# Two of a head's three half-filled filter blocks share one block of 128 rows, with operand tiles made by transfers within SBUF

## What is computed

```python
x = x + _L0_conv_ref(_gn(x), gate_w, w1, w2, w3)         # experts
x = x + _L1_conv_ref(_gn(x), w3, w7, w15, w_mix)         # and two more like it
...
x_flat = x.reshape(b, l, h * d).transpose(0, 2, 1)
outs = [_causal_dwconv(x_flat, w) for w in (w3, w7, w15)]
y = jnp.concatenate(outs, axis=1)
y = y.reshape(b, h, n_scales * d, l).transpose(0, 3, 1, 2)
return jnp.einsum('blhm,dm->blhd', y, w_mix)
```

## Time and profile before

| | us |
|---|---|
| median of 3 runs | 1094.27 (1093.65 to 1095.57) |
| profiled execution: its own time | 1094.17 |
| its span in the profile | 1092.2 |
| PE (TensorE matmul) busy in the span | 1040.1 (95%) |
| DVE, ACT, POOL busy | 501.0, 318.4, 126.3 |

### The profile page before, as it was taken

The page is one execution under the profiler, slowest core; times in us unless marked ns, Lnnn a source line. Parts: engine busy times, 40 slices in busy tenths (PEclk is TensorE's granted clock), DMA queues, the critical chain, the costliest instruction groups (busy, mean ns, idle before and its releaser), DMA issues.

```text
span 1092.2 us, 14489 instructions
## 1 busy us (share of the span) xinstructions
PE 1040.1 (95%) x5315; PEld 870.7 (80%) x5316; DVE 501.0 (46%) x700; ACT 318.4 (29%) x435; POOL 126.3 (12%) x169
## 2 busy tenths in 40 slices
PE   5589999999999999999999999779999999999998
PEld 3278888888888888888888888668888988898887
DVE  4794154155136155245164372266236942587011
ACT  2412144144144244144144352114201320122122
POOL 2031111111111211111111122100000000000000
PEclk9859999999999999999999999979999999999999
DMA  8309216943972985953976949755373466436474
GB/s 346 126 20 340 48 29 241 390 158 145 389 253 68 399 320 213 393 183 116 410 269 259 392 149 400 241 216 186 128 231 132 148 231 224 148 117 246 153 222 116
DMA packets 69792, 240.16 MB, mean 220 GB/s; under 512 B 6272, under 2 KB 36096, under 8 KB 55360
## 3 DMA queue, kind: packets, MB, share of 16 engines
q1 hardware_dynamic: 61536, 216.62, 52.1%
q0 software_dynamic: 8080, 23.07, 9.0%
q10 hardware_dynamic: 144, 0.02, 0.0%
HBM read 136.15 MB, written 107.74 MB: 223 GB/s over the span
## 4 chain that ended last, share of the span: by engine, by line
PE 83%; DVE 7%; issue 4%; DMA 3%; SPq 1%; ACT 1%; POOLq 0%; DVEq 0%; ACTq 0%; POOL 0%
PE gate_ps L977 15%; PE up_ps L977 15%; PE y_ps L964 10%; PE head_ps L1466 9%; PE head_ps L1470 9%; PE head_ps L1467 9%; PE y_ps L967 5%; PE hT_ps L989 2%; PE xT_ps L954 1%; PE xT_ps L886 1%; SPq L409 1%; DMA block_row<-in_x,fetch 1%; DVE scaled L1267 1%; DVE split L1277 1%; PE turn_ps L1416 1%
## 5 line engine op out<-in xcount | busy, mean ns | idle before, releaser
L1466 PE MATMUL head_ps<-split,ring 128*128 128x256 f32 (+1 forms) x657 | 225.4, 343 | 1.4 <-ACT split L1158 1.2
L1470 PE MATMUL head_ps<-split,ring 128*128 128x256 f32 (+1 forms) x657 | 220.6, 336 | 0.0
L1467 PE MATMUL head_ps<-split,ring 128*128 128x256 f32 (+1 forms) x657 | 220.1, 335 | 0.0
L977 PE MATMUL gate_ps<-front 128*128 128x512 f32 x560 | 177.3, 398 | 1.8 <-DVE xT_lo L810 1.7
L977 PE MATMUL up_ps<-front 128*128 128x512 f32 x560 | 173.8, 392 | 0.0
L1466 PEld LDWEIGHTS head_ps<-split,ring 128*128 128x128 f32 x657 | 124.4, 189 | 15.4 <-issue 2.1
L1470 PEld LDWEIGHTS head_ps<-split,ring 128*128 128x128 f32 x657 | 124.3, 189 | 14.6
L1467 PEld LDWEIGHTS head_ps<-split,ring 128*128 128x128 f32 x657 | 124.6, 190 | 13.6
L827 DVE TENSOR_TENSOR hidden<-silu,up_ps 128x1024 f32<-128x1024 f32 x35 | 42.8, 1222 | 177.9 <-ACT silu L586 177.9
L977 PEld LDWEIGHTS up_ps<-front 128*128 128x128 f32 x560 | 105.7, 189 | 22.9
L977 PEld LDWEIGHTS gate_ps<-front 128*128 128x128 f32 x560 | 102.9, 189 | 22.2 <-DVE xT_lo L810 2.1
(11 more groups left out here) (189 smaller groups left out, 1164.7 us busy)
## 6 DMA issues: line engine op xcount, KB each, us to landing
filters<-rows SPq DMA_DIRECT2D x56, 1568.0 KB
w_raw<-in_w13T SPq DMA_DIRECT2D x32, 1024.0 KB, 7.1
ring<-filters SPq DMA_DIRECT2D x15, 1920.0 KB, 7.9
w_raw<-in_w2T SPq DMA_DIRECT2D x16, 1024.0 KB, 5.2
ring<-filters SPq DMA_DIRECT2D x21, 768.0 KB, 4.7
ring<-filters SPq DMA_DIRECT2D x12, 1152.0 KB, 6.0
rows<-in_x SPq DMA_DIRECT2D x4, 1024.0 KB, 8.1
rowed<-acc SPq DMA_DIRECT2D x4, 1024.0 KB, 6.1
```

Source lines behind the costliest of these rows:

```text
L977: last = nc.tensor.matmul(o[:, n, :], a[:, k, :], b[:, k, t, n * 512:(n + 1) * 512], start=(k == 0 and a is xT_hi and b is w13_hi), stop=( ...
L1466: nc.tensor.matmul(place, kernel_hi, x_hi, start=(u == 0 and a == 0), stop=False)
L1467: nc.tensor.matmul(place, kernel_lo, x_hi, start=False, stop=False)
L1470: last = nc.tensor.matmul(place, kernel_hi, x_lo, start=False, stop=(u == len(units) - 1 and a == windows(s) - 1))
```

## The change

A head's three units end with a half-filled block each. Two of them (units 0 and 1, for head 5 units 1 and 2, which have the same scale) give their last blocks to one block of 128 rows: the upper half of one filter block stays in partitions 64 to 127, that of the other is loaded into partitions 0 to 63. The moving operand of that block, `shared`, is put together in the same way from the two groups' `split`: partitions 64 to 127 of the one stay, those of the other go to 0 to 63. This is done by transfers from SBUF to SBUF, issued by POOL: 2 for a task of 512 columns, 4 for a task of 256. Four slots of `shared` are used in turn. Each head now has one block less, three matmuls; the shared block comes last in the task. SP issues two loads more for each head (the two halves of its shared block), and where the parts of a run are no longer equally long, one more. The ring has 36 places instead of 48, at new positions. DVE gets one more memset, of the zero columns of `shared`.

```diff
+def head_shared(h):
+    units = head_units(h)
+    return (0, 1) if units[0][0] == units[1][0] else (1, 2)
+
+def head_parts(h):
+    return [(s, j, windows(s) - (m in head_shared(h))) for m, (s, j) in enumerate(head_units(h))]
...
 def head_windows(h):
-    return sum(windows(s) for s, _ in head_units(h))
+    return sum(n for _, _, n in head_parts(h)) + 1
...
-RING = 48
-RING_PLACE = {11: 0, 12: 15, 6: 30, 13: 0, 14: 15, 15: 30, 10: 0, 7: 15, 8: 30, 9: 39, 0: 0, 1: 6, 2: 15, 3: 24, 4: 30, 5: 36}
+RING = 36
+RING_PLACE = {11: 0, 12: 14, 6: 28, 13: 0, 14: 14, 15: 0, 10: 14, 7: 28, 8: 0, 9: 16, 0: 8, 1: 24, 2: 0, 3: 14, 4: 19, 5: 28}
...
+SHARED = 4
+SHARED_AT = {h: i % SHARED for i, h in enumerate(HEAD_ORDER)}
+SHARED_PARTS = {None: (slice(0, 2),), 0: (slice(0, 1), slice(1, 2)), 1: (slice(0, 1), slice(1, 2))}
...
+        shared = sb("shared", [P, SHARED, 2, BATCH, LEAD + P], f32r)
...
+                at = (RING_PLACE[h] + head_windows(h) - 1) * 2 * P
+                for half, m in zip((1, 0), head_shared(h)):
+                    s, j, count = head_parts(h)[m]
+                    begin = SCALE_AT[s] + count * P
+                    sp.dma_start(ring[half * P // 2:(half + 1) * P // 2, at:at + 2 * P].bitcast(f32).rearrange("p (a n) -> p a n", n=P),
+                                 filter_rows[P // 2:P, 2 * (l * GROUPS + j):2 * (l * GROUPS + j + 1), begin:begin + P]).then_inc(ring_in[h], 16)
...
+        @block.gpsimd
+        def _(pool):
+            def share(n):
+                l, h, pair = TASKS[n]
+                slot, bs = SHARED_AT[h], batches(pair)
+                piece = l * len(PIECES) + max(PIECE_OF[head_units(h)[m][1], pair] for m in head_shared(h)) + 1
+                pool.wait_ge(high_ok, piece)
+                pool.wait_ge(low_ok, piece)
+                if SHARED_AFTER[n] is not None:
+                    pool.wait_ge(head_done, SHARED_AFTER[n])
+                for half, m in zip((1, 0), head_shared(h)):
+                    j = head_units(h)[m][1]
+                    for parts in SHARED_PARTS[pair]:
+                        pool.dma_start(shared[half * P // 2:(half + 1) * P // 2, slot, parts, bs.start:bs.stop, LEAD:LEAD + P].bitcast(f32),
+                                       split[P // 2:P, j, parts, bs.start:bs.stop, LEAD:LEAD + P].bitcast(f32)).then_inc(shared_in[slot, pair], 16)
+
+            for n in range(len(TASKS)):
+                share(n)
...
-                    for a in range(windows(s)):
+                    for a in range(count):
...
+                a = head_parts(h)[head_shared(h)[0]][2]
+                kernel_hi, kernel_lo = (ring[:, (2 * at + part) * P:(2 * at + part + 1) * P] for part in range(2))
+                x_hi, x_lo = (shared[:, SHARED_AT[h], part, bs.start:bs.stop, LEAD - a:LEAD - a + P] for part in range(2))
+                pe.wait_ge(shared_in[SHARED_AT[h], pair], 16 * SHARED_COUNT[n])
+                nc.tensor.matmul(place, kernel_hi, x_hi, start=False, stop=False)
+                nc.tensor.matmul(place, kernel_lo, x_hi, start=False, stop=False)
+                last = nc.tensor.matmul(place, kernel_hi, x_lo, start=False, stop=True)
```

More of the change, by code:

```diff
@@ L1050, in conv_part @@
         ring_in = [sem(f"ring_in{h}") for h in range(HEADS)]
+        shared_in = {(n, pair): sem(f"shared_in{n}_{pair}") for n in range(SHARED) for pair in (0, 1, None)}
         lane_step = sem("lane_step")
@@ L1244, in lane_steps @@
                 nc.vector.reciprocal(lane_rstd[:, PAIR * pair:PAIR * (pair + 1)], lane_std[:, :]).then_inc(lane_step, 1)
+                if pair == 0:
+                    nc.vector.memset(shared[:, :, :, :, 0:LEAD].bitcast(f32), 0.0).then_inc(split_zeroed, 1)
             def take_spread(pair):
@@ L1447, in head @@
                 if n == 0:
-                    pe.wait_ge(split_zeroed, 1)
+                    pe.wait_ge(split_zeroed, 2)
                 pe.wait_ge(ring_in[h], 16 * RING_COUNT[i])
@@ L1454, in head @@
                 at = RING_PLACE[h]
-                units = head_units(h)
-                for u, (s, j) in enumerate(units):
+                for u, (s, j, count) in enumerate(head_parts(h)):
                     if u:
@@ L1469, in head @@
                             pe.wait_ge(low_ok, piece)
-                        last = nc.tensor.matmul(place, kernel_hi, x_lo, start=False, stop=(u == len(units) - 1 and a == windows(s) - 1))
-                    at += windows(s)
+                        nc.tensor.matmul(place, kernel_hi, x_lo, start=False, stop=False)
+                    at += count
+                a = head_parts(h)[head_shared(h)[0]][2]
[5 more added lines that the diff above has]
+                last = nc.tensor.matmul(place, kernel_hi, x_lo, start=False, stop=True)
                 last.then_inc(head_done, 1)
```

21 lines of the change are left out of this document (13 added, 8 removed).

## The result

The change makes the kernel slower. Its median is 1135.20 us (1130.33 to 1143.66, 4 runs) against 1094.92 us (1093.65 to 1095.64, 4 runs) of the kernel before, timed beside it, a ratio of 1.0374 with a 95% interval of 1.0326 to 1.0422. Predicted were 1070 us and a range of 1063 to 1087, so both the value and the range missed, on the other side of the old time. The profiled execution took 1130.33 us, with a span of 1128.6.

A forecast was written before the change was run, and what follows sets the result against it. The prediction took PE to bound whole tasks, and PE and DVE both to be at their limit at the second layer's beginning; 24.7 + 0 - 0.7 + 0 = 24.0 us off 1094.17 gave 1070 us, range 1063 to 1087.

The forecast's parts named there:

- Everything else I cost at nothing: Whole tasks' transfers, SP's additional loads, the memset of zeros and PE's 66 more waits were put at 0 us.
- The ring rival: Head 12's filter blocks, for task 23, come late from the smaller ring; task 23 ends 3.0 us later: 1076 us, chance 0.06.
- POOL as the bound: Tasks 16 to 27 and 38 to 49: POOL's 48 transfers in a row set the pace; 1125 us at 1.61 each, chance 0.12.
- DVE holds up POOL: In the transitions each transfer waits for a DVE instruction, up to 1.1 us each: 1078 us, chance 0.20.
- The heads have 1773 matmuls at an unchanged pace: Sign that the prediction is right: 1773 matmuls of heads at an unchanged pace.
- the predicted 0.7 less: Whole tasks: three matmuls fewer make each 0.705 us shorter.
- The 24.7 us of the safe tasks: Tasks between the transitions, 29 whole and 12 half ones, gain 20.4 + 4.3 = 24.7 us.
- the sum of 24.0: Total gain forecast for the kernel: 24.7 + 0 - 0.7 + 0 = 24.0 us.
- The transitions: Tasks 0 to 5, 19 to 27 and 41 to 50: transfers decide how much of 9.3 us of removed matmuls is gained.
- where 0.7 was said: Task 50, third layer's beginning: PE waits longer for ACT's first copy and the moved block costs 0.7 us.
- the first rival: The transitions keep half of their 9.3 us because transfers land in little over 1 us: 1065 us, chance 0.10.
- The 0 for the layers' beginnings: Beginnings of the layers gain 0 us; in the second, one transfer wait at task 23's end takes nine tasks' 3.2 us.

The follow-up runs named there:

- without transfers: The changed kernel without its 204 transfers and PE's waits for them, POOL zeroing the shared tile instead (shared block's result left out): 1070.74 us, ratio 0.9784 to the kernel before.
- POOL's copies: The change with both halves of the shared tile copied by POOL in place of all transfers: 1074.91 us, ratio 0.9834 to the kernel before.
- Over 128 partitions: The long pieces' kernel (change with zero columns copied too), each transfer carrying one part over 128 partitions, not both over 64 (wrong data): 1077.41 us, ratio 0.9849.
- the kernel with both kinds: The long pieces' kernel (change with zero columns copied too), staying half copied by POOL, crossing half by transfer: 1082.58 us, ratio 0.9906 to the kernel before.

## Why the prediction was wrong

**The step that failed** is "Everything else I cost at nothing". It priced a transfer as POOL's time to issue it and its time to land in an empty machine, and never its time on the DMA engines, which ring loads share. The sum had no term for 25.2 MB; they took 116 us of engine time, and with the transfers in place the kernel took 64 us longer than without them. The row that should have raised the question was quoted: in whole tasks the DMA engines' share was 0.63 before the change, and of the two shares the prediction used only the 0.06 of the row above it. The term can be worked out for the ten tasks 28 to 37. Before, the ring's loads take 0.60 x 71.9 = 43.1 us of the engines. Twenty transfers of 262,144 bytes are 5.24 MB. At the 408 GB/s of a burst of loads they take 12.9 us more, at the 217 GB/s that was measured 24.2. The tasks were to take 65.0 us. The first gives a share of 56.0 / 65.0 = 0.86, which would have left the forecast standing; the second gives 67.3 / 65.0 = **1.03**, more than there is. (The new kernel's loads are a little less, 0.61 x 65.04 = 39.7 us without transfers, which makes it 0.98, still above the 0.90 that was harmless.) So two things were missing, the term and the rate of a 64-partition transfer. The section of the Trainium skill that states this rate ("SBUF — State Buffer", "Door 1: The DMA port swizzle") was not weighed. Even so the sum would have been short: the ring loads' own packets became longer too, by 37.4 us over the whole kernel.

**The ring rival had the right place and the wrong price.** "The ring is late" looked at head 12 alone, with landings of 6.1 to 12.6 us from a trace in which no transfers competed. PE waited for a load at the start of thirteen tasks. Line 1135 loads a head's whole blocks, line 1141 the halves of its shared block. The landings of line 1135 and then of line 1141 in the change:

```profile
DMA to landing us min/median/max: 3.8/7.2/14.5
```
```profile
DMA to landing us min/median/max: 5.7/8.7/18.7
```

and the same two without transfers:

```profile
DMA to landing us min/median/max: 2.8/4.5/11.6
```
```profile
DMA to landing us min/median/max: 2.6/4.3/11.5
```

The rival's chance of 0.06, and its 1076 us, came from a landing taken as a constant.

**POOL as the bound** (0.12, the only slower case) did not happen: the issues take 0.59 to 0.70 us where 1.3 was its turning point. The value taken, 0.68, lies between the median, 0.595, and the longest, 0.702. A slower outcome was given 0.12 for a reason that the trace contradicts.

**DVE holds up POOL** (0.20) did not happen for transfers: their longest issue in 204 is 0.702 us, and 70 of them ran beside DVE's normalising instructions with both operands in SBUF. The rule weighed there (the Trainium skill, "SBUF — State Buffer", "Who interferes with whom") held both ways: plain transfers are not slowed, and POOL's copies, which read SBUF, collide with DVE's two-operand instructions, 978 in place of 692 ns.

**What was right.** The heads have 1773 matmuls at an unchanged pace; without transfers a whole task such as task 29 takes 9.92 us where it took 10.59, the predicted 0.7 less. The 24.7 us of the safe tasks stand once the transfers are gone. The profiled execution of that kernel took 1070.37 us, 23.8 less than the 1094.17 of before, but that it lies so near the sum of 24.0 is in part luck: the experts' part happened to end 1.3 us earlier in it, and the zeroing put task 0 back by 3.1.

**The transitions** were off in both directions. Without transfers PE gains 1.4 us from task 19 to 28, 1.4 from 41 to 50 and 2.6 from 0 to 6, and task 50 loses 3.9 (it goes from 13.0 to 16.9 us, its wait for ACT from 1.8 to 4.8) where 0.7 was said: the mechanism, PE arriving earlier at a fixed time, was right, the amount was not. In all they keep 1.5 us even with no transfer to wait for, so the first rival, which had 4.6, fails also. The 0 for the layers' beginnings came from a wait for the transfers, and is put to the test by a kernel that has them and room for them. Over 128 partitions the stretch from task 19 to 28 takes 37.9 us, where it took 36.5: a loss of 1.4, with its wait at the end of task 22.

**The budget.** From the kernel without transfers to the change the span grows by 59.9 us. PE's waits for DMAs are 46.3 of it, and the same matmuls take 21.3 us longer at the lowered clock; the rest goes the other way: waits like that of task 50 shrink.

## What to carry to other kernels

Price a new transfer on three clocks: the engine that issues it, its landing, and its bytes on the DMA engines; add the last to the share that the stretch already has, and expect everyone's landing times to grow when the sum comes near 1. In the ten tasks a share of 0.90 was harmless here; from 0.94 on 2.5 to 10.7 us were lost, where the matmuls saved 7. A transfer on 64 partitions ran at 0.6 to 0.75 of the rate of one on 128; for a few kilobytes of each row, a copy by an idle engine, even onto other partitions, was better than any transfer.

## What the runs showed of the hardware

- 64-partition transfers ran at 217 to 268 GB/s of engine time, whether from the same half, the other half or DRAM, and in SP's queue no faster (26.0 MB in 115 us, some 225); 128-partition ones at 358. Splitting one job over both halves in two transfers (1118.5 us) did not help.
- Packets of ring loads took longer beside the transfers: 237 us in the convolution part of the change, 199 without transfers, for the same loads.
- Halving the bytes with the number of transfers kept, and halving both, gave 1074.8 and 1077.5 us: POOL's 66 additional issues were free, with POOL busy for 18% of the span.
- A `tensor_copy` on POOL can move 64 partitions onto the other 64, at the speed of one that stays: in the kernel with both kinds the medians are 0.62 us each for a half task and 1.06 each for a whole one.
- A `memset` by POOL of 128 x 4224 numbers, 3.62 us long, made a DVE instruction beside it take 4.15 us in place of 1.28.
- PE's granted clock went from 1.00 (2.4 GHz) to 0.50 (1.2 GHz) during gaps of 3.0 to 6.6 us in the change, and after the one ahead of task 8 it was still 0.50 for 4 us, in which matmuls came every 0.4 us and more in place of 0.235.
